# Layer norms of a fused window-attention and convolution kernel: from tokens-by-channels with batch statistics to channels-by-tokens with centred weights, a matmul of ones, Ln and Exp

## The reference

```python
def layernorm(x, g, b):
    mu = jnp.mean(x, -1, keepdims=True)
    var = jnp.var(x, -1, keepdims=True)
    return (x - mu) * jax.lax.rsqrt(var + EPS) * g + b
...
xa = self_attention(xh, sa_wq, sa_wk, sa_wv, sa_wf, sa_bf)   # x + attention(x) @ wf + bf
xa = layernorm(xa, ln_self_g, ln_self_b)
...
q = cross_attention(attn_list[idx - 1], kv, ca_wq, ca_wk, ca_wv, ca_wf, ca_bf)
q = layernorm(q, ln_cross_g, ln_cross_b)
...
res = jax.nn.relu(q @ ffn_w1 + ffn_b1) @ ffn_w2 + ffn_b2
out = layernorm(q + res, ln_out_g, ln_out_b)
...
y = conv3x3(sign(clip(out)), sign(weight))     # then batch-normalised per channel
return out + y
```

## Time and profile before

| | us |
|---|---|
| median of 3 runs | 2700.24 |
| lowest, highest | 2686.36, 2701.25 |
| the profiled execution | 2692.97 |
| its span, first to last instruction | 2691.2 |

### The profile page before, as it was taken

One profiled execution on the slowest core, in us unless ns is written; L12 is line 12 of the kernel. 1 busy time (PEld: TensorE's weight loads), 2 busy tenths in 40 slices (PEclk: granted clock), 3 DMA queues, 4 the chain that ended last, 5 costly groups with the idle time before them and its releaser, 6 DMA issues.

```text
span 2691.2 us, 68616 instructions
## 1 busy us (share of the span) xinstructions
PE 2260.2 (84%) x27032; PEld 1774.8 (66%) x27032; DVE 1637.2 (61%) x5101; ACT 1420.7 (53%) x2531; POOL 1035.6 (38%) x1080
## 2 busy tenths in 40 slices
PE   5887878999799988999799988999799998999700
PEld 4666666777677766777677766777677766777500
DVE  4776665666466665667566665666566655545332
ACT  3654555555366655666466654565456554445332
POOL 3433434443344343444344443444344544443100
PEclk9998999999799999999899998999799999999955
DMA  4553444444244433444244433444334433323077
GB/s 104 130 125 92 122 100 103 109 111 107 75 111 110 110 96 96 109 110 113 77 112 112 109 96 87 112 107 107 82 103 110 112 94 83 80 72 82 19 234 262
DMA packets 387234, 288.26 MB, mean 107 GB/s; under 512 B 61537, under 2 KB 326498, under 8 KB 386914
## 3 DMA queue, kind: packets, MB, share of 16 engines
q1 hardware_dynamic: 386066, 282.88, 40.0%
q10 hardware_dynamic: 848, 0.99, 0.1%
HBM read 69.87 MB, written 56.46 MB: 47 GB/s over the span
## 4 chain that ended last, share of the span: by engine, by line
PE 56%; DVE 17%; SPq 10%; DMA 9%; issue 3%; ACT 3%; POOL 1%; POOLq 0%; ACTq 0%; DVEq 0%
PE ps_y L656 8%; SPq L408 8%; PE ps_hid L645 8%; PE ps_proj L511 6%; PE ps_o L593 5%; PE ps_max L566 4%; PE ps_s L580 4%; PE ps_hid L675 4%; PE ps_s L575 3%; DVE onorm L885 3%; PE ps_y L612 2%; PE ps_y L625 2%; DVE xn L927 2%; PE ps_t L606 2%; SPq L422 2%
## 5 line engine op out<-in xcount | busy, mean ns | idle before, releaser
L1033 POOL TENSOR_TENSOR prob_lo<-prob,prob_hi 128x512 f16<-128x512 f32 x528 | 610.9, 1157 | 931.7 <-ACT prob_hi L744 931.6
L743 ACT ACTIVATE prob<-ps_s 128x512 f32<-128x512 f32 x528 | 315.1, 597 | 403.2 <-PE ps_s L580 401.5
L873 DVE TENSOR_REDUCE negmax<-ps_max 128x8 bf16<-128x512 f32 x528 | 360.3, 682 | 155.9 <-PE ps_max L566 154.5
L880 DVE RECIPROCAL rden<-ps_o 128x8 f32<-128x8 f32 x528 | 108.0, 205 | 548.6 <-PE ps_o L593 547.4
L566 PE MATMUL ps_max<-ks,qs 128*64 128x128 f16 x4224 | 328.2, 288 | 0.3 <-issue 0.2
L885 DVE TENSOR_TENSOR onorm<-ps_o,rden 64x128 f32<-64x128 f32 x1056 | 304.8, 289 | 25.6
L744 ACT ACTIVATE prob_hi<-ps_s 128x512 f16<-128x512 f32 x528 | 313.4, 594 | 0.0
L593 PE MATMUL ps_o<-vb,prob_hi 128*128 128x68 f16 x4224 | 295.1, 197 | 1.6 <-DVE onorm L885 1.6
L656 PEld LDWEIGHTS ps_y<-w_sb,hid 128*128 128x128 f32 x2048 | 266.2, 196 | 33.3 <-issue 28.5
L645 PE MATMUL ps_hid<-xf,w_sb 128*128 128x512 f32 x512 | 283.4, 636 | 3.0 <-ACT yconv L801 2.1
L656 PE MATMUL ps_y<-w_sb,hid 128*128 128x128 f32 x2048 | 277.3, 279 | 0.6 <-ACT hid L782 0.6
(11 more groups left out here) (107 smaller groups left out, 3705.3 us busy)
## 6 DMA issues: line engine op xcount, KB each, us to landing
qs<-q_flat SPq DMA_DIRECT2D x1024, 64.0 KB, 2.5
ks<-k_flat SPq DMA_DIRECT2D x1024, 64.0 KB, 2.7
vb<-v_flat SPq DMA_DIRECT2D x128, 136.0 KB, 2.4
vb<-values_out SPq DMA_DIRECT2D x128, 136.0 KB, 2.8
xin<-in_x SPq DMA_DIRECT2D x64, 256.0 KB, 3.3
self_out<-xa SPq DMA_DIRECT2D x64, 256.0 KB, 2.9
xin<-self_out SPq DMA_DIRECT2D x64, 256.0 KB, 3.3
ffn_out<-x SPq DMA_DIRECT2D x64, 256.0 KB, 2.5
```

Source lines behind the costliest of these rows:

```text
L743: activation(prob[:, pair_no(u, k) % 2, :], ps_s[:, :], ACT.Exp)
L873: v.tensor_reduce(negmax[:, pair_no(u, k) % 2, :], ps_max[:, :].rearrange("p (a t) -> p a t", t=TOK), AX.X, ALU.max, negate=True).then_inc ...
L1033: g.tensor_tensor(prob_lo[:, i, :], prob[:, i, :], prob_hi[:, i, :], ALU.subtract).then_inc(s_prob, 1)
```

## The change

The norms are computed with channels on the partitions, as the tokens lie. Centring over channels is a matrix: the residual becomes a matmul with (identity - 1/128) as stationary operand, and the output projection and the second feed-forward matrix are multiplied by the same matrix once at the start (seven small matmuls, copied by DVE), as is the bias. So ps_y holds the centred sum; ACT squares it with the bias added, one matmul with a matrix of 1/128 gives the variance in every channel's row (into ps_t), ACT takes Ln(variance + eps) and Exp(-0.5 x that) for a root r0. One Newton step follows: DVE (variance + eps) x r0 and (y + bias) x r0, POOL times r0, DVE (that - 3) x (y r0). The factor -0.5 is in the gain (gain_h) of ACT's affine step, which now reads SBUF. The transposes `residual`, `spread` and `turn_out`, the bias matmul, the statistics, the four applies and POOL's power are gone. The table set of ACT is loaded ahead by name. The low units use the flat tiles q_flat, k_flat, v_flat of the main ones, so that `v_hi` waits for the move of the v before it for them too. `step0` frees ps_y and ps_t. The tables have new places for these stages and others; in LOW the output projection moves from 3.2 to 3.6 and the key and value stages by one slot, in CROSS out_store from 14.4 to 15.0 and conv from 14.6 to 15.6.

```diff
 SELF = dict(load=-10.3, q=-7.8, q_hi=-7.6, q_lo=-7.45, q_move=-7.0, k=-6.8, k_hi=-6.6, k_lo=-6.45, k_move=-6.0,
-            v=-5.8, v_hi=-5.6, v_lo=-5.45, v_move=-5.0, turn=4.16, turned=4.24, resid=5.2, project=6.2,
-            stats=6.5, rstd=6.55, apply=6.9, spread=7.56, spread_out=7.66, store=8.0, pool=8.6)
+            v=-5.8, v_hi=-5.6, v_lo=-5.45, v_move=-5.0, turn=4.1, turned=4.2, project=5.1, square=5.35,
+            var=5.75, log=5.85, root=5.9, step0=6.3, step1=6.45, norm=7.2, affine=7.45, store=7.9, pool=8.6)
...
+        bias_c = sb("bias_c", [128, 3])
+        gain_h = sb("gain_h", [128, 3])
...
+        ident, centre, mean = consts_sb[:, 0:128], consts_sb[:, 128:256], consts_sb[:, 256:384]
...
             def project_out(u):
+
+                n = u.pairs * C
+                if y_no["project", u.seq, None] > 1:
+                    pe.wait_ge(s_y_taken, y_no["project", u.seq, None] - 1)
+                mm(ps_y[:, 0:n], centre, tokens_of(u), start=True, stop=False, skip_group_check=True
+                   ).then_inc(s_resid, 1)
                 pe.wait_ge(s_t_taken, turn_no["turn", u.seq, None])
-                for p in range(u.pairs):
-                    done = mm(ps_y[:, C * p:C * p + C], oT[:, C * p:C * p + C], wf_sb[:, which(u), :],
-                              start=False, stop=True, skip_group_check=True)
-                done.then_inc(s_y, 1)
-
-            def spread(u):
-                turn_free("spread", u)
-                for p in range(u.pairs):
-                    pe.wait_ge(s_xn, xn_done[u.seq] - u.pairs + p + 1)
-                    done = mm(ps_t[:, C * p:C * p + C], xn[:, C * p:C * p + C], ident[:, :], is_transpose=True,
-                              start=True, stop=True, skip_group_check=True)
-                done.then_inc(s_t, 1)
+                mm(ps_y[:, 0:n], wfc_sb[:, which(u), :], oT[:, 0:n], start=False, stop=True,
+                   skip_group_check=True).then_inc(s_y, 1)
+
+            def variance(u):
+                turn_free("var", u)
+                n = u.pairs * C
+                pe.wait_ge(s_sq, y_no["project", u.seq, None])
+                mm(ps_t[:, 0:n], mean, sq[:, 0:n], start=True, stop=True, skip_group_check=True).then_inc(s_t, 1)
...
             def ffn_out_part(u, b):
+                if b == 0:
+                    if u.no:
+                        pe.wait_ge(s_y2_taken, u.no)
+                    mm(ps_y2[:, :], centre, xf[:, u.no % 2, :], start=True, stop=False, skip_group_check=True)
                 pe.wait_ge(s_hid_taken, hid_no[f"h{b}", u.seq, None])
-                for p in range(PAIRS):
-                    done = mm(ps_y2[:, C * p:C * p + C], hid[:, b % 2, C * p:C * p + C], w2_sb[:, b, :],
-                              start=False, stop=(b == FB - 1), skip_group_check=True)
-                done.then_inc(s_f, 1)
-
-            def turn_out(u):
-                turn_free("out", u)
-                for p in range(PAIRS):
-                    pe.wait_ge(s_xn2, PAIRS * u.no + p + 1)
-                    done = mm(ps_t[:, C * p:C * p + C], xn2[:, C * p:C * p + C], ident[:, :], is_transpose=True,
-                              start=True, stop=True, skip_group_check=True)
-                done.then_inc(s_t, 1)
+                mm(ps_y2[:, :], w2c_sb[:, b, :], hid[:, b % 2, :], start=False, stop=(b == FB - 1),
+                   skip_group_check=True).then_inc(s_f, 1)
...
+            def variance2(u):
+                turn_free("var2", u)
+                pe.wait_ge(s_sq2, u.no + 1)
+                mm(ps_t[:, :], mean, sq2[:, :], start=True, stop=True, skip_group_check=True).then_inc(s_t, 1)
...
+            def square(u):
+                n, m, at = u.pairs * C, which(u), y_no["project", u.seq, None]
+                act.wait_ge(s_y, at)
+                if at > 1:
+                    act.wait_ge(s_xn, at - 1)
+                activation(sq[:, 0:n], ps_y[:, 0:n], ACT.Square, bias=bias_c[:, m:m + 1]).then_inc(s_sq, 1)
+
+            def log(u):
+                act.wait_ge(s_t, turn_no["var", u.seq, None])
+                n = u.pairs * C
+                activation(sq[:, 0:n], ps_t[:, 0:n], ACT.Ln, bias=eps).then_inc(s_log, 1)
+
+            def root_of(u):
+                n = u.pairs * C
+                act.wait_ge(s_log, y_no["project", u.seq, None])
+                activation(root[:, 0:n], sq[:, 0:n], ACT.Exp, scale=-0.5).then_inc(s_root, 1)
...
-                activation(to, ps_t[:, 0:u.pairs * C], ACT.Identity, bias=shift[:, m:m + 1],
-                           scale=gain[:, m:m + 1]).then_inc(s_t_taken, 1)
+                activation(to, xn[:, 0:u.pairs * C], ACT.Identity, bias=shift[:, m:m + 1],
+                           scale=gain_h[:, m:m + 1]).then_inc(s_xa, 1)
...
+            nc.scalar.preload_act_table_set("natural_log_exp_and_others")
...
+            def step0(u):
+                n, m, at = u.pairs * C, which(u), y_no["project", u.seq, None]
+                dve.wait_ge(s_root, at)
+                v.scalar_tensor_tensor(out=sq[:, 0:n], in0=ps_t[:, 0:n], scalar=EPS, in1=root[:, 0:n], op0=ALU.add,
+                                       op1=ALU.mult).then_inc(s_t_taken, 1)
+                if at > 1:
+                    dve.wait_ge(s_xa, at - 1)
+                v.scalar_tensor_tensor(out=xn[:, 0:n], in0=ps_y[:, 0:n], scalar=bias_c[:, m:m + 1], in1=root[:, 0:n],
+                                       op0=ALU.add, op1=ALU.mult).then_inc(s_y_taken, 1)
+
+            def norm(u):
+                n, at = u.pairs * C, y_no["project", u.seq, None]
+                dve.wait_ge(s_step, at)
+                dve.wait_ge(s_y_taken, at)
+                v.scalar_tensor_tensor(out=xn[:, 0:n], in0=sq[:, 0:n], scalar=-3.0, in1=xn[:, 0:n],
+                                       op0=ALU.add, op1=ALU.mult).then_inc(s_xn, 1)
...
+            def step1(u):
+                n = u.pairs * C
+                pool.wait_ge(s_t_taken, turn_no["var", u.seq, None])
+                g.tensor_tensor(sq[:, 0:n], sq[:, 0:n], root[:, 0:n], ALU.mult).then_inc(s_step, 1)
```

More of the change, by code:

```diff
@@ L61 @@
-LAST_CONV = dict(conv=15.6, conv_take=15.9, conv_stats=16.2)
+             turn=4.1, turned=4.2, project=5.1, square=5.35, var=5.75, log=5.85, root=5.9, step0=6.3, step1=6.45,
+             norm=7.2, affine=7.45, h0=8.2, relu0=8.4, h1=9.2, relu1=9.4, h2=10.2, f0=10.38, f1=10.42,
+             relu2=10.45, h3=11.2, f2=11.35, relu3=11.4, f3=12.25, square2=12.4, var2=12.8, log2=12.9, root2=12.95,
+             step02=13.3, step12=13.45, norm2=14.2, out_take=14.5, out_store=15.0, conv=15.6,
+             conv_take=15.9, conv_stats=16.2)
@@ L139, in attention_conv @@
             last["k"] = u
-        if stage == "v" and u.kind == "self":
+        if stage == "v":
             before_v[u.seq] = last.get("v")
             last["v"] = u
-    before_turn, before_spread, before_resid = {}, {}, {}
+    before_var = {}
     for stage, u, what in order:
-        for name, of in (("turn", before_turn), ("spread", before_spread), ("resid", before_resid)):
-            if stage == name:
-                of[u.seq] = last.get(name)
-                last[name] = u
-    xn_done = {}
-    for stage, u, what in order:
-        if stage == "apply":
-            xn_done[u.seq] = (max(xn_done.values()) if xn_done else 0) + u.pairs
-    resid_no = numbered("resid")
+        if stage == "var":
+            before_var[u.seq] = last.get("var")
+            last["var"] = u
     same_b = {}
@@ L362, in attention_conv @@
         conv_hid = {what: n for (stage, _, what), n in hid_no.items() if stage == "conv"}
-        out_turn = {u.no: turn_no["out", u.seq, None] for u in units if u.kind == "cross"}
         block = ctx.enter_context(nc.Block())
@@ L718, in v_hi @@
                 act.wait_ge(s_proj, proj_no["v", u.seq, None])
[L719 removed]
+                if before_v[u.seq] is not None:
                     act.wait_ge(s_v_moved[before_v[u.seq].b], 32 * moves[before_v[u.seq].seq])
```

272 lines of the change are left out of this document (112 added, 160 removed).

## The result

The changed kernel takes 2792.35 us (median of 4 runs, 2788.46 to 2800.36), against 2697.93 for the kernel before on the same chip: 1.036 of it, 95% interval 1.034 to 1.0385, slower by 94 us. The forecast was +23 us; 2792 is within its range of 2640 to 2800, near the end, and the size was wrong. The profiled execution has a span of 2786.5 us.

The account below looks back on a forecast made before the run. PE was taken to set the pace, busy 84%. Rounds +48, low units -16, cross units alone -15, self units alone +4 and tail some 2 made +23 on the profiled 2693: 2716 us, range 2640 to 2800.

Parts of the forecast that it names:

- the cross units alone: The 16 cross units at the end: more PE work against waits that go and idle time, -15 us (bounds 0 and -25).
- Five rounds: Repeating order of eight pairs in mid-run: a round goes from 34.4 to 35.4 us, +1.0, over 48 rounds +48.
- the self units alone: The 16 self units at the start: they leave PE idle anyway, so added work costs only +4 us.
- no load waits for them longer: 0: SP's queue: stores move with the affine steps but keep their place between the loads, costing 0.
- PE work, attention norm: On PE, centring, projection and variance take 2.78 us for 2.00 before, 0.78 more for each of 128 units.
- Waits that go: PE's three waits for DVE's normalised tile, 113.9 us: 63 in the rounds, 23 at low units, 27 in the end's cross units.
- Waits that come: New PE waits in a round: v, the second variance behind its square, the weighing behind DVE's steps; 1.1 us (bounds 0 and 2.7).
- ACT: ACT's busy time comes near 1820 us, from 1421 and 200 x 2.0.
- Rival 1: ACT's queue becomes the bound, scores waiting for exponentials: 0.4 us for each of 192 norms, +77, 2793 us; chance 0.20.
- rival 4: The change does not do what it says, Ln and Exp reloading ACT's tables in turn; no chance.
- Rival 2: DVE and POOL exclude each other at the norm's last step, its mean well over 0.75 us; 2746 us; chance 0.15.
- Rival 3: New waits are hidden and small gaps go with the old waits: a round of 33.8 us, 2623 us; chance 0.25.

Follow-up runs that it names:

- e1: Changed kernel with a unit's load moved ahead of the eight q moves of the unit before it (-11.05 for -10.3): 2697.85 us, 1.0031 of the kernel before.
- e3: The kernel before the change, with the same early load (-11.05 for -10.3): 2668.12 us, 0.9912 of the kernel before.
- e4: Changed kernel, load late, with squares and the variance matmul in f16 instead of f32: 2665.24 us, 0.991 of the kernel before.
- e6: Changed kernel with the early load and with squares and the variance matmul in f16: 2595.09 us, 0.9665 of the kernel before.
- e10: Changed kernel with the early load and the second norm's variance, log and root moved behind the scores (13.06 to 13.08): 2647.84 us, 0.9872 of the kernel before.
- e8: Changed kernel with the early load and without the Newton step, one DVE operation per norm staying: 2643.59 us, 0.9847 of the kernel before.
- e2: Changed kernel, load late, with the last step's second tile kept in PSUM instead of SBUF: 2792.57 us, 1.0379 of the kernel before.
- e5: Changed kernel with the early load and the last step's second tile kept in PSUM: 2699.04 us, 1.0053 of the kernel before.

## Why the prediction was wrong in size

**The sum against the kernels with the load early.** There the change costs 29.7 us, for 23 forecast. By the marks, e1 against e3: until the first feed-forward norm 383.9 against 369.8, +14 (forecast +4); from there to the 48th 1820.6 against 1792.6, +28 (forecast +48 - 16 = +32); the cross units alone 346.1 against 357.4, -11 (forecast -15). Five rounds, in the place where the prediction took its 34.4, are 34.9 each in e1 and 34.45 in e3 (L664 from 1036.90 to 1209.15): +0.5 for +1.0. The plain rounds among them are 34.94 and 33.84, +1.1; e3 has two of 35.3 and 35.5 there, e1 none. By these marks the self units alone cost 10 us more than forecast, the rounds with the low units 4 less, the cross units 4 more; why the self units cost more even so I have not traced.

**The step that failed** is the one on the ring, in two sentences of the prediction: "Self units alone: they leave PE idle anyway, +4", and on SP "no load waits for them longer: 0". The first took idle time of PE as cover. It was idle inside a ring, and there the added work lengthened the ring: the stage took 41 us more for the 4 forecast. The second asked only whether the moved stores delay a load. It didn't ask what the load itself stands behind, and who releases that: the q moves, released by scores of PE, ahead of which the centring, the projection and the variance had been put. What it missed is what the early load gives the changed kernel more than the one before: by the marks 42 - 15 = 27 us in the self units and 51 - 14 = 37 in the rounds, 64 together; by the medians 94 - 19 = 75. The loss of 94 less the 29.7 that stay is 65; beside the kernel before as measured with e1 to e3 (2687.45) the loss is 105, and less the same 29.7 that is the 75.

**PE work, attention norm**: 2.76 us for 2.78, right. e4 and e6 show that 0.88 of such work reaches the end with the load late, 0.71 with it early.

**Waits that go**: all three of the earlier trace rows are gone. Right.

**Waits that come**: named right (v, the second square, the weighing behind DVE's steps), 1.1 us in a round by forecast. The second square costs 0.5 each time in the rows above, as forecast. The weighing's wait for onorm is 17.7 us over 31 places, about the 0.6 each forecast; but e10 and e8 show that removing them gives 50 and 54 us, more than the 33 and 37 us that these waits show. Other waits fell with them: all that the view lists add up to 268 us in e1, 226 in e10 and 221 in e8, and PE is busy 7 and 8 us less. A wait's own length is no upper bound for what its removal brings.

**ACT**: 1789 us busy for 1820 forecast; square, log and root under 0.70. Rival 1 did not happen: scores wait 11.9 us for prob_hi in all. That the measured 2792 is just the 2793 priced for it is chance. Nor did rival 4: the trace of the changed kernel has one table load.

**Rival 2** happened on DVE and not at the end. L910's mean is 1.18 us, well over the 0.75 that I had set as its sign; the exclusion takes 63 us on DVE, and in e2 and e5, which take it away and hold ps_y longer for it, the end gains nothing of them. The Trainium skill, "SBUF — State Buffer", section "SBUF: two separate sides", holds here in its mechanism: two inputs in SBUF wait out the POOL operation, one does not. That its sign would be on the page of the profile and its price not, I had not foreseen, and had the total come out near the 2746 us that I gave it, the sign would have seemed to confirm it.

**Rival 3**, the waits hidden and the gaps gone, fell: e1 leaves v, the square and onorm with 106 us.

## What to carry to other kernels

Before work is costed at nothing because its engine idles, follow the idle time back to what releases it, and that again, until the chain ends or comes round to the engine itself; in such a ring added work lengthens the round, and here the idle time in it lowered the clock besides. A load has to stand in its queue ahead of whatever waits for the consumer of the load before it, and a change that adds work should be tried with that order mended, in both kernels. A step that frees a bank is not to be put behind one that waits.

## What was not expected of the hardware

- A DVE operation with two inputs in SBUF that starts during a prob_lo of POOL ends about 0.55 us after it (79 of 80): 1.41 us for 0.68, and up to 1.69. With one input in PSUM it is 0.68 beside the same POOL operations (the changed kernel and e2).
- Behind idle stretches of 1.2 and 1.9 us the granted clock was 0.50 from 165 to 167 us, and q took 1.86 us for k's 0.87. In the kernel before an idle of 1.14 us ahead of q (at 174.00) left it at 1.00. I had priced PE's waits by their length alone.
- The variance in f16 is 0.22 us for 512 columns, in f32 0.94.
